# A layer norm with nodes on partitions, and one block for seven pooling layers, in a four-network graph kernel

## The reference, cut to what matters

```
h = relu(layernorm(x));  x = x + L0(h)      # two layers
h = relu(layernorm(x));  x = x + L1(h)      # four "sage" layers
h = relu(layernorm(x));  x = x + L2(h)      # one pooling with edge features, an MLP with three norms
h = relu(layernorm(x));  x = x + L3(h)      # two "conv" layers
# a sage layer:   h = h @ Ws + (segment_sum(h[src], dst) / max(deg, 1)) @ Wn + b   (relu after the first three)
# L2:             pools the rows of h and 32 edge features to the receiving nodes, then W1, norm, W2, norm, sum, norm
# a conv layer:   h = elu(segment_sum(norm * (h @ W)[src]) + b)
```

## Time and profile before

| | |
|---|---|
| three runs, median (lowest to highest) | 3164.58 us (3162.3 to 3167.12) |
| the profiled execution | 3166.68 us |
| its span, first to last instruction | 3164.7 us |
| PE busy with matmuls | 2923.2 us, 92% of the span |
| DVE, ACT, POOL busy | 1059.1, 737.8, 1114.3 us |
| mean granted TensorE clock | 0.960 |

### The profile page before, as it was taken

How to read it: one execution, slowest core, us unless ns; L and a number is a source line. 1 busy time by engine, 2 the same in 40 slices (tenths; PEclk the granted TensorE clock), 3 DMA queues, 4 the chain that set the end, 5 groups by cost and what they waited for, 6 DMA issues and landing times. The chain is left out here.

```text
span 3164.7 us, 44178 instructions
## 1 busy us (share of the span) xinstructions
PE 2923.2 (92%) x18659; PEld 1726.1 (55%) x18659; DVE 1059.1 (33%) x1877; ACT 737.8 (23%) x1183; POOL 1114.3 (35%) x1011
## 2 busy tenths in 40 slices
PE   1699969998799959999999999999799999999998
PEld 1688835554344415555555555555356665555554
DVE  5899922223300162111111111111523544222122
ACT  4799912213200041000000000000201543001000
POOL 5000013331000002563554565366076301671564
PEclk6899979998899979999999999999899999999999
DMA  7134599995466406666666666666365445665665
GB/s 267 41 124 133 179 227 169 179 167 92 114 151 145 89 0 207 182 182 166 178 178 163 180 178 175 168 175 172 101 185 161 120 116 139 181 185 156 171 169 159
DMA packets 769295, 492.61 MB, mean 156 GB/s; under 512 B 362660, under 2 KB 749996, under 8 KB 768624
## 3 DMA queue, kind: packets, MB, share of 16 engines
q1 hardware_dynamic: 706290, 395.76, 51.7%
q0 software_dynamic: 30112, 62.69, 6.8%
q10 hardware_dynamic: 32702, 31.44, 3.2%
HBM read 334.89 MB, written 76.82 MB: 130 GB/s over the span
## 5 line engine op out<-in xcount | busy, mean ns | idle before, releaser
L2327 PE MATMUL acc<-tbuf,hs 128*128 128x448 fp8e4 x8232 | 1606.7, 353 | 5.8 <-PEq L1242 3.1
L2301 POOL DMA_INDIRECT grow<-hrows,glist x882 | 942.9, 1069 | 899.7 <-DMA hrows<-hs 362.9
L2327 PEld LDWEIGHTS acc<-tbuf,hs 128*128 128x128 f16 x8232 | 801.1, 98 | 739.1 <-issue 34.8
L2659 DVE TENSOR_TENSOR edge_loc<-iota,gdl 128x768 f16<-128x768 bf16 x147 | 139.9, 956 | 729.9 <-PE acc L2356 669.3
L711 ACT ACTIVATE stage<-quad 128x784 fp8e4<-128x784 f32 x392 | 290.0, 828 | 8.2 <-PE quad L731 5.4
L1627 PE MATMUL acc<-tbuf,hs 128*128 128x512 fp8e4 (+1 forms) x1300 | 281.4, 370 | 11.2 <-DMA tbuf<-table 11.2
L731 PE MATMUL quad<-K,S 128*128 128x196 bf16 x1568 | 277.1, 249 | 15.7 <-DVE K L655 10.6
L735 PE MATMUL deg<-K,S 128*128 128x196 bf16 x1568 | 275.9, 247 | 0.0
L1500 PE MATMUL acc<-tbuf,hs 128*128 128x512 fp8e4 (+1 forms) x1300 | 267.3, 369 | 0.7 <-issue 0.7
L2549 ACT ACTIVATE H<-B,vectors 128x448 f32<-128x448 f32 (+2 forms) x56 | 37.4, 668 | 810.5 <-DVE B L2699 810.5
L1500 PEld LDWEIGHTS acc<-tbuf,hs 128*128 128x128 f16 x1300 | 123.6, 98 | 144.3 <-issue 4.1
(11 more groups left out here) (299 smaller groups left out, 1946.1 us busy)
## 6 DMA issues: line engine op xcount, KB each, us to landing
tbuf<-table SPq DMA_DIRECT2D x294, 448.0 KB
tbuf<-table SPq DMA_DIRECT2D x294, 336.0 KB
table<-stage SPq DMA_DIRECT2D x6, 5488.0 KB
hrows<-hs SPq DMA_DIRECT2D x34, 448.0 KB
grow<-hrows,glist POOLq DMA_INDIRECT x882
feat<-in_edge_attr_dram ACTq DMA_DIRECT2D x27, 448.0 KB, 6.3
C<-factors ACTq DMA_DIRECT2D x2, 3136.0 KB, 12.5
table<-stage SPq DMA_DIRECT2D x2, 2744.0 KB
```

What stands on the lines that cost most here:

```text
L2301: g.indirect_dma_start(out=grow[:, n % 2, t, :], out_offset=None, in_=k.hrows[l % 2], in_offset=bass.IndirectOffsetOnAxis(k.glist[:, i // ...
L2327: mm = T.matmul(acc(s, h), rows[l % 2][:, g * US + r, part, :], counts[:, (r - lo) * STRIP + h * HALF:(r - lo) * STRIP + (h + 1) * HALF], ...
L2659: V.tensor_tensor(hot[:, n % 2, :, :], k.iota[:, 0:P].unsqueeze(1).to_broadcast([P, GH, P]), k.gdl[:, i // GU, i % GU * GH:(i % GU + 1) * ...
```

## The change

The two calls of `layer_chain` become one over seven layers: sage 0 to 3, plain (number 4), conv 5 and 6. The blocks `layer_norm` and `split_rows` between them are no longer called here. The norm is computed inside the chain instead, group by group over `CHUNKS` (fourteen groups of four or three blocks, in the order in which strips leave), with nodes on partitions. In slot *it* (places in `NORM_ENTRIES`: eleven in the last sage layer, the other four in strip 0 of the plain layer):

- DVE computes the reciprocal root and shift of group it-1, adds the sage output to x for group it, writes the low half of group it-1; once PE has transposed group it into `bankN` (bank 4) it takes the statistics, writes x with nodes on partitions back to `A` with the bias row added, and aggregates.
- PE transposes x of group it (`norm_ask`), behind a wait for ACT's rows of group it-1; some pieces later it transposes the normed rows of group it-1 back (`norm_answer`, `bankZ`, bank 5).
- ACT takes the root for group it-1, writes the normed rows straight from `bankN` (relu with scale and shift), the high half, and copies the transposed-back rows to `H`.

SP stores the rows strip by strip, and loads the edge sums in seven pieces during strip 0 of the plain layer. The transposes of x in `answer`, with DVE's addition to them, leave the plain layer's MLP. The plain layer's units move from `unit_places(6, 27)` to `unit_places(12, 24)`: the first at piece 12 instead of 6, the last at piece 60 as before. The set-up of the second chain (small loads, constants, bias parts, the degrees' transpose) moves to the start of the one chain.

```diff
@@ half_pieces and tables @@
+NORM_ENTRIES = [(1, 3), (1, 6), (2, 3), (2, 6), (3, 3), (3, 6), (4, 1), (4, 4), (4, 7), (5, 3), (5, 6)]
+NORM_SLOTS = NG + 1
...
+NORM_ASK, NORM_ANSWER = half_pieces(NORM_ENTRIES, NORM_SLOTS, NSAGE - 1, 1)
...
-EARLY_UNITS = unit_places(6, 27)
+EARLY_UNITS = unit_places(12, 24)
@@ layer_chain, sync @@
+                for g in range(NG):
+                    l, s, i, h = [at for at, it in NORM_ASK.items() if it == g + 1][0]
+                    n = (l * DENSE + s) * NH + i + R + (2 if l == plain else 3)
+                    if CHUNKS[g][1]:
+                        stores[n] = (plain - 1, g)
...
+                edges = {plain * DENSE * NH + R + 1 + 2 * s: s for s in range(NU)}
...
+                    if n in edges:
+                        s = edges[n]
+                        sp.wait_ge(acc_read.h, acc_read.at(plain * len(CHUNKS)))
+                        sp.dma_start(k.C[0:3 * DE, s * STRIP:(s + 1) * STRIP],
...
@@ layer_chain, tensor @@
-                    g = in_flight(it, 0)
-                    if g is not None:
-                        if n_of["Z"]:
-                            pe.wait_ge(dve_lo.h, dve_lo.at(n_of["Z"]))
                         if g:
-                            pe.wait_ge(dve_X.h, dve_X.at(g))
-                        turned_back(bankZ, g, lambda b, i: A[:, block_at(b, i)], pe_X)
...
+                def norm_ask(g):
+                    if g < NG:
+                        b, n = group_blocks(g, CHUNKS)
+                        pe.wait_ge(n_added.h, n_added.at(g + 1))
                         if g:
+                            pe.wait_ge(n_y.h, n_y.at(g))
...
+                        for i in range(n):
+                            mm = T.transpose(bankN[:, i * P:(i + 1) * P], A[:, block_at(b, i)], k.idf[:, :])
+                        mm.then_inc(n_turned.h, 1)
+
+                def norm_answer(g):
+                    if g >= 0:
+                        n = group_blocks(g, CHUNKS)[1]
+                        pe.wait_ge(n_y.h, n_y.at(g + 1))
+                        if g:
+                            pe.wait_ge(n_H.h, n_H.at(g))
+                        for i in range(n):
+                            mm = T.transpose(bankZ[:, i * P:(i + 1) * P], y[:, i * P:(i + 1) * P], k.idf[:, :])
+                        mm.then_inc(n_back.h, 1)
...
+                            elif l and s == 0 and normed(l - 1):
+                                if i % 2 == 0:
+                                    src = max(n for n, c in enumerate(CHUNKS) if c[0] == PIECES[i][0])
+                                    pe.wait_ge(n_lo.h, n_lo.at(src + 1))
@@ layer_chain, scalar @@
+                def norm_step(g):
+                    ...
+                    act.wait_ge(n_stats.h, n_stats.at(g + 1))
+                    A_.activation(n_rs[:, g % 2, 0:n], n_mv[:, g % 2, 0:n, 1], ACT.Sqrt, bias=k.eps[:, 0:1]
+                                  ).then_inc(n_std.h, 1)
+                    act.wait_ge(n_roots.h, n_roots.at(g + 1))
+                    ...
+                    for i in range(n):
+                        ins = A_.activation(y[:, i * P:(i + 1) * P], bankN[:, i * P:(i + 1) * P], ACT.Relu,
+                                            scale=n_rs[:, g % 2, i:i + 1], bias=n_sh[:, g % 2, i:i + 1])
+                    ins.then_inc(n_y.h, 1)
+                    ...
+                    act.wait_ge(n_back.h, n_back.at(g + 1))
+                    A_.activation(H[:, group_cols(g, CHUNKS)], bankZ[:, 0:n * P], ACT.Copy).then_inc(n_H.h, 1)
@@ layer_chain, vector @@
-                    if gX is not None:
-                        n, at = group_blocks(gX)[1], group_cols(gX)
-                        dve.wait_ge(pe_X.h, pe_X.at(gX + 1))
-                        V.tensor_tensor(blocks(A[:, at], n), blocks(bankZ, n), wide(2, n), ALU.add).then_inc(dve_X.h, 1)
...
+                def norm_step(it):
+                    ...
+                        link(V.reciprocal(rs_g, rs_g))
+                        V.scalar_tensor_tensor(sh_g, n_mv[:, g % 2, 0:n, 0], -1.0, rs_g, ALU.mult, ALU.mult
+                                               ).then_inc(n_roots.h, 1)
+                    ...
+                        V.tensor_tensor(A[:, at], A[:, at], v[:, at], ALU.add).then_inc(n_added.h, 1)
+                    ...
+                        V.scalar_tensor_tensor(to[:, :, 1, :], blocks(y, n), scale(0, plain), to[:, :, 0, :],
+                                               ALU.mult, ALU.subtract).then_inc(n_lo.h, 1)
+                    ...
+                            ins = V.bn_stats(n_st[:, i, :], bankN[:, i * P:(i + 1) * P])
+                        link(ins)
+                        V.tensor_tensor(blocks(A[:, at], n), blocks(bankN, n), wide(2, n), ALU.add)
+                        for i in range(n):
+                            ins = V.bn_aggr(n_mv[:, g % 2, i, :], n_st[:, i, :])
+                        ins.then_inc(n_stats.h, 1)
@@ network @@
-                layer_chain(k, H, B, layers, range(2, 6), tbuf, factor=1)
...
+                layer_chain(k, H, B, layers + [("plain",)] + [("conv", W[f"g{l}"], vec(24 + l)) for l in range(2)],
+                            (2, 3, 4, 5, 0, 6, 7), tbuf, out, w)
+            return
```

More of the change, by code:

```diff
@@ L2025, with half_pieces @@
 ENTERS = [0, 1, 2, 3, 4, 5, 6, None, 7, 8, 9, None, 10, 11, None, None, None, 12, 13] + [None] * LAG_Z
-def half_pieces():
+NORM_ENTRIES = [(1, 3), (1, 6), (2, 3), (2, 6), (3, 3), (3, 6), (4, 1), (4, 4), (4, 7), (5, 3), (5, 6)]
+NORM_SLOTS = NG + 1
+NSAGE = 4
+def half_pieces(entries, slots, l, first):
     ask, answer = {}, {}
-    for it in range(len(ENTERS)):
-        if it < len(ENTRIES):
-            s, i = ENTRIES[it]
-            ask[0, s, i, 0], answer[0, s, i + 1, 1] = it, it
-        else:
-            n = 3 * (it - len(ENTRIES))
-            ask[1, 0, n // 2, n % 2], answer[1, 0, (n + 2) // 2, n % 2] = it, it
+    for it in range(slots):
+        if it < len(entries):
+            s, i = entries[it]
+            ask[l, s, i, 0], answer[l, s, i + 1, 1] = it, it
+        else:
+            n = first + 3 * (it - len(entries))
+            ask[l + 1, 0, n // 2, n % 2], answer[l + 1, 0, (n + 2) // 2, n % 2] = it, it
     return ask, answer
-ASK, ANSWER = half_pieces()
+ASK, ANSWER = half_pieces(ENTRIES, len(ENTERS), NSAGE, 0)
+NORM_ASK, NORM_ANSWER = half_pieces(NORM_ENTRIES, NORM_SLOTS, NSAGE - 1, 1)
 def unit_places(first, step):
@@ L2106, in slot_of, with layer_chain @@
     return ENTERS.index(g)
-def layer_chain(k, v, dst, layers, scale_at, tbuf, factor=None, out=None, w=None):
+def layer_chain(k, v, dst, layers, scale_at, tbuf, out, w):
     nc = k.nc
@@ new lines, in _ @@
+                for g in range(NG):
+                    l, s, i, h = [at for at, it in ASK.items() if it == slot_of(g) + LAG_Z][0]
+                    n = (l * DENSE + s) * NH + i + R + (1 if l > plain else 3)
+                    while n in stores:
+                        n += 1
+                    if GROUPS[g][1] or g >= NG - 2:
+                        stores[n] = (plain, g)
+                    if GROUPS[g][1]:
+                        l, s, i, h = [at for at, it in ASK.items() if it == slot_of(g)][0]
+                        factors[(l * DENSE + s) * NH + i + R + 2] = g
@@ L2548, in replace @@
                         act.wait_ge(moved.h, moved.at(nth(l, s, q)))
-                        A_.activation(v[:, at], dst[:, at], layers[l][3], bias=layers[l][4]).then_inc(ready.h, 1)
+                        A_.activation(v[:, at], dst[:, at], layers[l][3], bias=layers[l][4]).then_inc(ready["sage"].h, 1)
                     if l in convs:
@@ L2688, in leave_bank @@
                         dve.wait_ge(used.h, used.at((l * DENSE + s + 1) * NH))
-                    if l in sages and l != sages[0]:
-                        dve.wait_ge(ready.h, ready.at(nth(l - 1, s, q)))
+                    if l and l - 1 in sages:
+                        dve.wait_ge(ready["sage"].h, ready["sage"].at(nth(l - 1, s, q)))
                     if kinds[l] == "plain":
@@ L3333, in network @@
         with table_buffer(k, True) as tbuf:
-            split_rows(k, H, True, 0, None, None, tbuf, False, not spilled)
-            if spilled:
-                pool_neighbours(k, B, None, None, tbuf, False, H, None, 0)
-            else:
-                layer_chain(k, H, B, [("plain",)] + [("conv", W[f"g{l}"], vec(24 + l)) for l in range(2)], (0, 6, 7), tbuf,
-                            out=out, w=w)
+            split_rows(k, H, True, 0, None, None, tbuf, False)
+            pool_neighbours(k, B, None, None, tbuf, False, H, None, 0)
         rest(k.spill_rows, k.spill_src, k.spill_dst, D, H, B)
-        for l in range(2 if spilled else 0):
+        for l in range(2):
             weight = W[f"g{l}"]
```

249 lines of the change are left out of this document (139 added, 110 removed).

## The result

| | before | after |
|---|---|---|
| median (lowest to highest) | 3165.52 us (3162.3 to 3167.12) | 3115.89 us (3110.67 to 3116.63) |
| profiled execution, span | 3166.68, 3164.7 us | 3115.19, 3113.6 us |
| PE busy with matmuls | 2923.2 us, 92% | 2884.4 us, 93% |
| mean granted clock | 0.960 | 0.964 |

The ratio is 0.9843, 95% interval 0.983 to 0.9855: the change gains 49.6 us, and 3117 was forecast. That the sum came out so near is partly luck: two terms were off in opposite directions, and the executions differ ahead of the change by up to 8 us.

A forecast was written before the change was run, and what follows sets the result against it. PE was taken to set the time in the chains, with a 59.35 us border without pieces between them. 60.8 - 5.3 - 0 - 5.0 - 3.8 + 1.0 = 47.7 us faster: 3117 us against the median, eight-in-ten range 3105 to 3138.

The forecast's parts named there:

- The border: Between sage and plain layers: 59.35 us without pieces and 1.4 us of cold start go, together 60.8 us gained.
- Transposes: On PE: the norm transposes 49 blocks twice, the MLP's transposes of x go once; 5.3 us net lost.
- Slots in the last sage layer: Norm work on DVE and ACT lies beside PE's pieces: no wait, bounds 0 and 5.5 us.
- Slots in strip 0: Plain layer's strip 0: PE waits 2.0, 1.1 and 1.8 us for normed rows, sum 5.0 us, bounds 0 and 17.
- The first gathers: Plain layer's first two units wait 2.1 and 1.7 us, the last strip's store standing behind a load; 3.8 us, bounds 0 and 12.
- The MLP: Plain layer's MLP: DVE loses fourteen additions and PE as many waits; 1 us gained, bounds 0 and 7.4.
- A: Rival: longer waits in strip 0, gathers and last sage layer, five costing 2.8 us of clock each; 3136 us, chance 0.18.
- B: Rival: nothing waits at slots or gathers, and the MLP's 7.4 us go too; 63 us gained, 3102 us, chance 0.12.
- C: Rival: each of fourteen norm groups pays its whole 4.3 us chain in PE's way; slower, 3172 us, chance 0.05.
- D: Rival: POOL's later gathers in the plain layer bound it and eat the gain; 3162 us, chance 0.03.
- a late load of edge sums: Plain layer: would delay the MLP's first products by no more than the two gather waits have already given.

The follow-up runs named there:

- e3: Kernel before with the norm block between the two chains left out, edge sums and row of ones still loaded; ratio 0.9906, median 3136.25 us.
- e5: Changed kernel with the two DVE masks at the plain layer's start moved behind the roots of slot 11; ratio 0.9825, chain measure 1369.47 us.
- e6: Changed kernel with the store of the norm's last strip issued two pieces earlier on SP's queue; ratio 0.9816, median 3107.30 us.
- e2: Kernel before without the MLP's own transposes of x and DVE's 14 additions behind them; ratio 0.9942, median 3148.53 us.
- e8: Kernel before with DVE's addition of the MLP's turned x placed ahead of its step's roots, nothing left out; ratio 0.9977, median 3158.65 us.
- e7: Changed kernel with both edits, masks behind the roots and last store two pieces earlier; ratio 0.981, median 3104.74 us.
- e10: Kernel of e9 with the plain layer's two masks built behind the roots of the last turned group; ratio 0.9801, median 3104.82 us.
- e9: Kernel of e7 with ACT's copy of a turned-back group into H moved behind the next group's rows; ratio 0.9825, chain measure 1362.84 us.
- e4: Changed kernel with DVE taking each group's norm statistics twice, same result; ratio 0.9836, median 3111.43 us.

## Why the prediction was right, and where it was not

- *The border, +60.8.* It went: no stretch without pieces is left. e3 adds what the prediction didn't ask, that only half of it was the norm.
- *Transposes, -5.3.* The last sage layer loses 8.3 us (75 at 0.11), strip 0 another 2.5, and x's own give back 5.4: -5.4.
- *Slots in the last sage layer, 0.* Right: its 8.3 us are the transposes', and the view has no wait there.
- *Slots in strip 0, -5.0.* 1.82, 0.94 and 1.67, in all 4.4, for 2.0, 1.1 and 1.8 (which are 4.9). The chains were those named; e5 shows that behind the masks there was a second one, ACT's, 0.7 us shorter.
- *The first gathers, -3.8.* Too small: 7.0 us of waits and 1.7 of half clock, and in the changed kernel's second profile 5.8 and 1.3. Counted from the sage layers' last matmul, the first gather came at 35.1 us for 33.9, the first unit's products at 45.3 for 44.4, and PE stood ready at 42.3, as worked out: 3.0 of wait for 2.1. The second wait was 2.5 for 1.7. Each is a small difference between two long sums, of which the gathers' was one us too low. Two waits of 0.7 to 0.8 in strip 2 and the clock were not in the sum. e6 shows the cause where the prediction had it, in the store behind piece loads on SP.
- *The MLP, +1.0.* This is the step that failed. The prediction put it that PE waited "for reasons other than a named engine" and took 1 of the 7.4 us. e2 measures 13.6 us beside the transposes, 8.3 in waits and the rest in clock. What the view put down to "issue" was the wait for DVE's addition, which in the longest case ended 0.1 us before; e8, which moves the addition alone, halves the waits. That the earlier trace rows showed one such wait with the half clock behind it, priced in the prediction at 2.8 us, should have put at least 7.4 and 2.8 into the term, since the change removes what was waited for.

With the measured terms: 60.8 - 5.4 - 4.4 - 8.7 + 13.6 = 55.9, where the chain measure has 54.8. Against that the forecast of 47.7 was 7 us short; that the medians moved by only 49.6 hides it, and that part of the hit is luck.

*The rivals.* A priced each of five waits with 2.8 us of clock. The three slots, 1.82, 0.94 and 1.67 us within 14 us, cost no clock (1.00 from 2246.40 to 2270.00); the pair at the gathers, 3.01 and 2.51 us, did behind its second wait. The Trainium skill (TensorE: Matmul & The Clock Gate, "A second HAM failure mode: psum-queue depth-cycling") says that frequent short idling between groups of matmuls makes the clock swing; by the traces here that held for the pair and not for the slots. B took the MLP's 7.4 us and was right there, wrong in having no waits. C and D didn't occur: no group paid its whole chain, and the layer's last unit is on no wait. The prediction held that a late load of edge sums costs no more than the gathers' waits have already given. That was so in the profile after; in the changed kernel's second one the MLP's first products wait 0.55 us beside them, in e7 1.66.

## What to carry to other kernels

A wait that a view puts down to "issue" is somebody's: look which instruction of another engine, or which load, ended just before it ends, and whether the change removes it. Price a wait with the clock behind it, from rows at either level, and allow for both outcomes: here one wait of 2.34 us cost 1 us of clock in some executions and none in others. Where a block between two streams is dissolved, count the restart of the second stream (its store, its first gathers) as well as the block's own work, and look then at what comes last there: here a store queued behind loads was worth 5.3 us at the gathers, while waits removed ahead of it were worth nothing (e5, e10) or about 1 us (e7, e9).

## What was not expected of the hardware

The same code ahead of the chain took between 1206.37 and 1214.63 us in thirteen profiles. What a wait does to the clock does not go by its length alone: the rows behind waits of 3.27 us (before), 3.46 (the changed kernel's second profile), 4.25 (e4) and 2.65 (e10) are slow, those behind 2.21 us (e8), 3.01 (after, the first unit) and 3.76 (e5, the first unit) are not. Nor by the code around it: behind the MLP's wait of 2.34 to 2.36 us the rows are slow in e3, e6 and e9 and at full speed before, after and in e2, e7 and e10. The store of the last strip had its gather behind it after 5.4 to 5.9 us in eight profiles, and after 7.2 in e10.
